# Decoder layer on one core: values' sums in three passes over rounded halves, normalisation on ScalarE, and the table scatters split over two steps

## The reference, cut to what matters

```python
theta_x = einsum('ld,bdt->btl', theta_w, input2) + theta_b
phi_x = einsum('ld,bdt->blt', phi_w, input1) + phi_b[:, None]
p = softmax(einsum('btl,bls->bts', theta_x, phi_x), axis=-1)   # 16 x 512 x 512
g_x = einsum('ld,bdt->btl', g_w, input1) + g_b
t_x = einsum('bts,bsl->blt', p, g_x)                           # the values' sums
# mean and variance of t_x over a whole batch, normalise, gamma, beta, relu
w_t = einsum('ol,blt->bot', out_w, relu(h)) + out_b[None, :, None] + input2
# then, per token: probs = softmax(norm(x) @ Wg), the top 2 of 8 experts, and a
# place below the capacity of each; the place decides the row of a slot table
```

## Time and profile before

| | |
|---|---|
| median of 3 runs | 2969.3 us (2965.92 to 2970.14) |
| the profiled execution | 2979.34 us, its span 2977.6 us |
| mean granted PE clock in it | 0.973 of full |
| PE / DVE / ACT / POOL busy, share of the span | 95 / 42 / 29 / 29 % |
| chain that ended last | PE 61%, nearly all of it in the experts |

### The profile page before, as it was taken

The page is one execution under the profiler, slowest core; times in us unless marked ns, Lnnn a source line. Parts: engine busy times, 40 slices in busy tenths (PEclk is TensorE's granted clock), DMA queues, the critical chain, the costliest instruction groups (busy, mean ns, idle before and its releaser), DMA issues.

```text
span 2977.6 us, 46435 instructions
## 1 busy us (share of the span) xinstructions
PE 2825.9 (95%) x16374; PEld 2310.4 (78%) x16374; DVE 1245.7 (42%) x2129; ACT 870.0 (29%) x1681; POOL 873.7 (29%) x1330
## 2 busy tenths in 40 slices
PE   6989999998999966999999999999999999999998
PEld 6855555556665536999999999999999999999997
DVE  6756777646788752233132133133133133123111
ACT  1126666641544522222122122122122122112110
POOL 4546777622266662021021021021011011111110
PEclk9999999978999977999999999999999999999999
DMA  3101222232121214232033033033023023122110
GB/s 107 42 2 39 44 43 47 54 94 79 57 78 71 78 43 122 68 113 87 11 107 97 11 106 96 11 96 103 12 96 102 19 89 95 30 87 76 36 47 20
DMA packets 97076, 194.66 MB, mean 65 GB/s; under 512 B 22126, under 2 KB 23758, under 8 KB 96800
## 3 DMA queue, kind: packets, MB, share of 16 engines
q1 hardware_dynamic: 75072, 131.77, 14.8%
q0 software_dynamic: 21856, 60.73, 6.6%
HBM read 148.77 MB, written 38.94 MB: 63 GB/s over the span
## 4 chain that ended last, share of the span: by engine, by line
PE 61%; DMA 0%; POOL 0%; DVE 0%; issue 0%; ACT 0%; DVEq 0%; POOLq 0%
PE ex_hid L1751 30%; PE ex_acc L102 10%; PE ex_acc L103 10%; PE ex_acc L104 10%; PE ex_xb L1721 1%; DMA ex_ys<-xn_dram,ex_slot_gather 0%; POOL out_dram L1603 0%; POOL ex_ys L1583 0%; DVE ex_ys L1664 0%; POOL ex_xg L1568 0%; DMA ex_ys<-slot_table_dram 0%; PE ex_acc L1721 0%; DVE ex_h0l L1672 0%; ACT ex_h0h L1631 0%; DVE ex_xT0l L1647 0%
## 5 line engine op out<-in xcount | busy, mean ns | idle before, releaser
L1672 DVE SCALAR_TENSOR_TENSOR ex_h0l<-ex_hid,ex_h0h 128x640 fp32r<-128x640 f32 x128 | 105.6, 825 | 683.1 <-ACT ex_h0h L1631 683.1
L1672 DVE SCALAR_TENSOR_TENSOR ex_h1l<-ex_hid,ex_h1h 128x640 fp32r<-128x640 f32 x128 | 105.5, 824 | 602.8 <-ACT ex_h1h L1631 602.2
L1631 ACT ACTIVATE ex_h0h<-ex_hid 128x640 fp32r<-128x640 f32 x128 | 90.3, 705 | 734.8 <-PE ex_hid L1751 734.8
L1631 ACT ACTIVATE ex_h1h<-ex_hid 128x640 fp32r<-128x640 f32 x128 | 90.3, 705 | 729.6 <-PE ex_hid L1751 729.6
L654 DVE TENSOR_REDUCE at_nb<-at_ring 128x2 f32<-128x512 f32 (+1 forms) x384 | 246.8, 686 | 122.0 <-PE at_ring L760 122.0
L1573 POOL COPY ex_gi<-ex_slot_gather 128x1 int32 (+1 forms) x82 | 15.3, 186 | 916.5 <-PE ex_xb L1721 912.1
L102 PE MATMUL ex_acc<-ex_w_h,ex_h1h 128*128 128x512 f32 x640 | 254.5, 398 | 0.0
L102 PE MATMUL ex_acc<-ex_w_h,ex_h0h 128*128 128x512 f32 x640 | 253.1, 395 | 0.0
L103 PE MATMUL ex_acc<-ex_w_l,ex_h0h 128*128 128x512 f32 x640 | 250.5, 391 | 0.0
L103 PE MATMUL ex_acc<-ex_w_l,ex_h1h 128*128 128x512 f32 x640 | 250.4, 391 | 0.0
L104 PE MATMUL ex_acc<-ex_w_h,ex_h1l 128*128 128x512 f32 x640 | 249.8, 390 | 0.0
(11 more groups left out here) (271 smaller groups left out, 5831.3 us busy)
## 6 DMA issues: line engine op xcount, KB each, us to landing
ex_raw<-in_w_tiles_dram SPq DMA_DIRECT2D x256, 256.0 KB, 2.8
x_in<-in_x_dram SPq DMA_DIRECT2D x32, 256.0 KB, 2.6
act<-at_raw SPq DMA_DIRECT2D x128, 64.0 KB
at_recb<-o_rec_dram SPq DMA_DIRECT2D x16, 512.0 KB
k<-in_x_dram SPq DMA_DIRECT2D x32, 256.0 KB, 2.6
cx_ctx<-in_ctx_dram SPq DMA_DIRECT2D x16, 512.0 KB, 3.6
out_dram<-cx_res SPq DMA_DIRECT2D x16, 512.0 KB, 2.8
xn_dram<-cx_prob SPq DMA_DIRECT2D x16, 512.0 KB, 2.8
```

The lines of the kernel that those rows point to most:

```text
L1631: act.activation(h[f % 2][0][:], hid[:, :, 0:HB], ACT.Relu).then_inc(sm["h_hi"], 1)
L1672: dve.scalar_tensor_tensor(h[f % 2][1][:], hid[:, :, 0:HB], 0.0, f32(h[f % 2][0][:]), ALU.max, ALU.subtract).then_inc(sm["h_lo"], 1)
```

## The change

Values' sums: pT and g's copy are kept as rounded part and remainder (fp32r), the products become three passes; DVE makes the remainders. pT has one buffer instead of two. ACT scales the probabilities (`normalise`), DVE makes only the reciprocals. In odd steps `route_exp` stands ahead of `hid`; the routing's 1/sum moves from POOL's pow to a DVE reciprocal. A group's scatters: six in the even step, the last two in the next odd step after `group_root`. `residual` moves to the end of POOL's step. One more step pair is written out ahead of the loop. SP's program is unchanged.

```diff
-        pT = [s.sb(f"cx_pT{c}", [P, NTT, D]) for c in range(CB)]
+        pT = [s.sb("cx_pT", [P, 2 * NTT, D], F32R)] * CB
-        keys = [s.sb(f"cx_keys{c}", [P, D]) for c in range(CB)]
+        keys = [s.sb(f"cx_keys{c}", [P, 2, D], F32R) for c in range(CB)]
-        LINKS = 26
+        AT_ONCE = 6
+        LINKS = 25
@@ steps
             both(0)
-            with eng.Fori(1, groups - 2) as j:
+            both(1)
+            with eng.Fori(2, groups - 2) as j:
@@ POOL
-                wait_apart(pool, sm["route_exp"], GT * (g + 1), sm["passed_pool"])
-                link(g, TT(exsum[:], exsum[:], minus[:].to_broadcast([P, GT]), ALU.pow))
+                wait_apart(pool, sm["exsum"], g + 1, sm["passed_pool"])
@@ POOL step
                 if within(n - 1, 0, B):
                     group_root(n - 1, 1 - a)
-                if within(n, 0, B):
-                    residual(n, a, j + 1 - a)
+                if within(j - 2, 0, groups - 1) and a == 1:
+                    scatter(j - 2, range(AT_ONCE, TOPK * GT))
...
                 if routed and a == 0:
-                    scatter(j - 1, range(TOPK * GT))
+                    scatter(j - 1, range(AT_ONCE))
+                if within(n, 0, B):
+                    residual(n, a, j + 1 - a)
@@ ACT
+            def normalise(n, c, tiles):
+                for q in tiles:
+                    act.wait_ge(sm["rinv"], ONE + NTT * n + ORDER.index(q) + 1)
+                    act.activation(prob[c][:, q, :], prob[c][:, q, :], ACT.Copy, scale=rinv[:, c, q:q + 1])\
+                        .then_inc(sm["norm"], 1)
@@ ACT step
+                if this:
+                    normalise(n, a, EARLY)
                 if ahead:
                     latent_hi(n + 1, b, "phi")
+                if a == 1 and within(j - 1, 0, groups - 1):
+                    route_exp(j - 1)
                 if last:
                     act.wait_ge(sm["scaled"], ONE + n)
...
-                if a == 1 and within(j - 1, 0, groups - 1):
-                    route_exp(j - 1)
...
                     exponentials(n, a, j + 1 - a, LATE)
+                if this:
+                    normalise(n, a, LATE)
@@ DVE
+            def g_lo(n, c):
+                dve.wait_ge(sm["g_kept"], ONE + n + 1)
+                dve.tensor_tensor(keys[c][:, 1, :], bank[c][2][:], f32(keys[c][:, 0, :]), ALU.subtract)\
+                    .then_inc(sm["g_lo"], 1)
+            def pT_lo(n, c):
+                for q in range(NTT):
+                    dve.wait_ge(sm["pT"], ONE + NTT * n + q + 1)
+                    dve.tensor_tensor(pT[c][:, NTT + q, :], bank[c][q][:], f32(pT[c][:, q, :]), ALU.subtract)\
+                        .then_inc(sm["pT_lo"], 1)
+            def invert_sums(g):
+                wait_apart(dve, sm["route_exp"], GT * (g + 1), sm["passed_dve"])
+                dve.reciprocal(exsum[:], exsum[:]).then_inc(sm["exsum"], 1)
@@ DVE step (both normalise calls become invert_row: the reciprocal alone)
                     for q in LATE:
                         maximum(n, a, q)
+                if ahead:
+                    g_lo(n + 1, b)
+                if a == 1 and within(j - 1, 0, groups - 1):
+                    invert_sums(j - 1)
...
                 if ahead:
                     latent_lo(n + 1, b, "theta")
+                if this:
+                    pT_lo(n, a)
                 if last:
                     dve.wait_ge(sm["rstd"], ONE + n)
@@ PE (theta waits for g_lo instead of g_kept)
                     for q in range(NTT):
-                        pe.wait_ge(sm["pT"], ONE + NTT * n + q + 1)
-                        m = pe.matmul(bank[a][0][:], keys[a][:, q * P:(q + 1) * P], pT[a][:, q, :],
-                                      start=q == 0, stop=q == NTT - 1)
+                        pe.wait_ge(sm["pT_lo"], ONE + NTT * n + q + 1)
+                        m = split_passes(pe, bank[a][0][:], [keys[a][:, i, q * P:(q + 1) * P] for i in range(2)],
+                                         (pT[a][:, q, :], pT[a][:, NTT + q, :]), q == 0, q == NTT - 1)
```

More of the change, by code:

```diff
@@ L910, in stage_cross @@
         least = s.sb("rt_least", [P, E, E])
-        minus = s.sb("rt_minus", [P, 1])
         empty = s.sb("rt_empty", [ST, P, 2], I32)
@@ L920, in stage_cross @@
                  "phi_hi", "phi_lo", "g_kept", "scores", "neg_max", "exp", "rinv", "norm", "turned",
-                 "pT", "tx", "tx_kept", "row_stats", "row_moments", "row_sq", "row_m2", "all_moments",
+                 "pT", "pT_lo", "g_lo", "tx", "tx_kept", "row_stats", "row_moments", "row_sq", "row_m2", "all_moments",
                  "gmv", "gsq", "gvar", "gve", "grstd", "centred", "scaled", "hid", "out", "x2", "stats",
@@ L924, in stage_cross @@
                  "logits_kept", "empty", "consts", "linked", "route_exp", "chosen", "placing",
-                 "placed", "linked_last", "last_slots", "passed_dve", "passed_pe", "passed_pool")
+                 "placed", "exsum", "linked_last", "last_slots", "passed_dve", "passed_pe", "passed_pool")
         sm = {n: s.sem("cx_" + n) for n in names}
@@ L1003, in constants @@
                 pool.iota(empty[:, :, 1], pattern=[[0, P]], base=0, channel_multiplier=0).then_inc(sm["empty"], 1)
-                pool.memset(minus[:], -1.0).then_inc(sm["consts"], 1)
                 pool.memset(acc[:], 0.0).then_inc(sm["consts"], 1)
                 pool.memset(least[:], float(2.0 ** -126)).then_inc(sm["consts"], 1)
-                pool.wait_ge(sm["consts"], ONE + 5)
+                pool.wait_ge(sm["consts"], ONE + 4)
                 for e in range(E):
@@ L1011, in constants @@
                 pool.tensor_copy(tokenf[:], ti[:]).then_inc(sm["consts"], 1)
-                pool.wait_ge(sm["consts"], ONE + 15)
+                pool.wait_ge(sm["consts"], ONE + 14)
                 TS(ec[:], ef[:], float(CAP), None, ALU.mult).then_inc(sm["consts"], 1)
@@ L1015, in constants @@
                     TS(dump[:, k, :], tokenf[:], float(SLOTS + k * B * S), None, ALU.add).then_inc(sm["consts"], 1)
-                pool.wait_ge(sm["consts"], ONE + 18)
+                pool.wait_ge(sm["consts"], ONE + 17)
                 every = [P, NT, E]
@@ L1020, in constants @@
                        dump[:, k, :].unsqueeze(2).to_broadcast(every), ALU.subtract).then_inc(sm["consts"], 1)
-                pool.wait_ge(sm["consts"], ONE + 20)
+                pool.wait_ge(sm["consts"], ONE + 19)
             def route_rank(g):
@@ L1129, in keep_g @@
                 act.wait_ge(sm["g"], ONE + n + 1)
-                act.activation(keys[c][:], bank[c][2][:], ACT.Copy).then_inc(sm["g_kept"], 1)
+                act.activation(keys[c][:, 0, :], bank[c][2][:], ACT.Copy).then_inc(sm["g_kept"], 1)
             def exponentials(n, c, i, tiles):
@@ L1214, in maximum, with invert_row @@
                     .then_inc(sm["neg_max"], 1)
-            def normalise(n, c, q):
+            def invert_row(n, c, q):
                 dve.wait_ge(sm["exp"], ONE + NTT * n + ORDER.index(q) + 1)
                 dve.reciprocal(rinv[:, c, q:q + 1], rsum[:, c, q:q + 1]).then_inc(sm["rinv"], 1)
-                dve.wait_ge(sm["rinv"], ONE + NTT * n + ORDER.index(q) + 1)
-                dve.tensor_scalar(prob[c][:, q, :], prob[c][:, q, :], rinv[:, c, q:q + 1], None, ALU.mult)\
-                    .then_inc(sm["norm"], 1)
+            def g_lo(n, c):
[7 more added lines that the diff above has]
+                        .then_inc(sm["pT_lo"], 1)
             def keep_logits(n, c):
@@ L1255, in step @@
                     for q in EARLY:
-                        normalise(n, a, q)
+                        invert_row(n, a, q)
                 if last:
@@ L1363, in _ @@
                 xin_lo(c, c)
-            for name in ("phi", "theta"):
-                latent_lo(0, 0, name)
+            latent_lo(0, 0, "phi")
+            g_lo(0, 0)
+            latent_lo(0, 0, "theta")
             steps(dve, step)
@@ L1372, in theta @@
                 pe.wait_ge(ctx_loaded[c], ONE + 16 * i + 16)
-                pe.wait_ge(sm["g_kept"], ONE + n + 1)
+                pe.wait_ge(sm["g_lo"], ONE + n + 1)
                 for k in range(TPB):
```

## The result

The change made the kernel slower: 3013.7 us (median of 4 runs, 3010.52 to 3019.93) against 2967.6, a ratio of 1.0159 with a 95% interval of 1.0145 to 1.0172. (The kernel before has a fourth run here, so its median is 2967.6 and no longer 2969.3.) The forecast was 2970.4, the range ended at 2984.

A forecast was written before the change was run, and what follows sets the result against it. PE was taken to bound even steps, and its wait for `hid` behind POOL's scatters to lengthen odd ones. Even steps +3.0, odd -2.75, ends -4.75 and clock +5.6 gave +1 on 2969.3: 2970.4 us, range 2952 to 2984.

The forecast's parts named there:

- the even step's term: Even steps: DVE's remainders outweigh PE's 0.66 us saving, so each takes 19.95 us against 19.45, +3.0 over six.
- 5.6 for the clock: Odd steps: PE's longer idle may lower its clock; half of 2.77 us, taken as 1.4, in four of five steps.
- the other steps and both ends: Steps 0 and 1 -0.6, step 3 +0.1, step 14 0.45 less, step 15 3.8 less: -4.75 us together.
- `hid` and L1277: Odd step: L1277 falls to 0.75 us, `hid` is ready at +9.55, and PE's wait of 3.23 us goes.
- SP's three transfers: Odd step: context load, x2 store and xn3 store start together at +7.5, held until the even step's `residual` ends.
- I take 13.1: Odd step: first LATE exponential waits for both stores until 7.5 + 1.4 + 4.2 = +13.1, against +14.46 today.
- the bound of 14.1: Odd step: latest landing of the stores, 7.5 + 6.6 us, the 6.6 being one transfer of 1536 KB.
- costs POOL and DVE what it does today: Port shared by POOL and DVE, odd step: no added cost from the change.
- The values' passes: Values' sums on PE: twelve passes take 0.66 us less, but PE waits about 1.5 us for DVE's pT remainders in even steps.
- given back by `residual`: Odd step: the 2.5 us of two scatters moved out are offset by `residual` now standing ahead of the next `group_root`.
- rival A: Odd steps: PE's clock falls at the values' passes and transposes, 17.8 less 4.5: +13, 2982 us; chance 0.30.
- a gain elsewhere is not to be had: Whole kernel: the change touches only the stage at 728 to 1120 us, 392 us of a span of 2977.6.

## Why the prediction was wrong

The step that failed first is the even step's term. I gave the six even steps 0.5 us each, +3.0, and they took +19.0: the odd step's residual now ends inside them, so the same three transfers hold the late exponential, the passes begin with the first remainder and end later, a held square stands on PE's path, and in two of them the clock falls. Second, the odd step's transfers were sized too small, and third, the experts stood in no term and lost 14.2. By the forecast's own frame:

| part of the stage | before | after | change | forecast |
|---|---|---|---|---|
| six even steps, 2 to 12 | 116.3 | 135.3 | +19.0 | +3.0 |
| five odd steps, 5 to 13 | 119.7 | 127.3 | +7.6 | +2.85 (-2.75, and 5.6 for the clock) |
| the other steps and both ends | 162.7 | 160.8 | -1.9 | -4.75 |

These are 23.6 us over the forecast, 16.0 of them in the even steps. With the experts' 14.2 that is 37.8 of the 43 that the medians lie above it; the rest is no more than how far the profiled executions lie from their medians. (The ends of the range, 2952 and 2984, are 1 and 2 us wider than the words beside them give.)

The change put together, one step after another, from the table of versions (each within about 3 us, and in this order only):

| step | cross | experts |
|---|---|---|
| before | 398.7 | 1850.9 |
| pair written out | +2.2 | -1.6 |
| scatters split | -13.9 | +1.6 |
| ACT normalises | -13.6 | -1.2 |
| route's exponential and reciprocal | -3.2 | +0.2 |
| three passes | +20.2 | +12.4 |
| residual last | +33.0 | +2.8 |
| after | 423.4 | 1865.1 |

- **`hid` and L1277: right.** The wait went, `scaled` takes 0.74 us in all steps, `hid` is ready at +10.0 (9.55 forecast).
- **SP's three transfers: right in place, wrong in size.** They are issued at +7.3 to +8.5 as forecast. The exponential starts at +15.0; "I take 13.1" fails, and so does the bound of 14.1, which came from one transfer of 1536 KB. In step 11 three transfers started together landed in 4.3 (load), 4.9 and 6.4 us (the stores), where a load had 3.6 and a store 2.8 alone; from the load's issue to the exponential that is 7.7 us, and 9.3 in step 9. The estimate of 5.6 us by the Trainium skill ("DMA: Bandwidth & Descriptors", "Anatomy of one DMA") is further off than the row of 6.6; the skill gives that sum there for GpSimd's path, a condition that the prediction left out, and these transfers are SP's.
- **The even step was given no such wait: the largest omission.** I moved only the even step's residual. The odd step's lands in the even step at +1.8 to +4.2, its load and stores at +4.3 to +5.5, and the late exponential waits 1.3 us (974.62, +11.3). Of the ten waits for the stores five are in even steps, 9.5 of the 31.4 us.
- **The port: "costs POOL and DVE what it does today" failed.** The large operation was freed (2.83 to 0.74), but the small ones with two SBUF inputs now meet the residual: 1.90 us on PE's path to `avg` in even steps, 2.98 on POOL's path to `grstd` in odd ones, 0.16 before. PE's waits for the mean matmul's operand rose from 1.6 us in 1 to 5.4 in 6.
- **The values' passes: mechanism right, size off.** PE waits 1.4 us a step for the first remainder on average, as forecast (1.5), and up to 2.65. But I let the last remainder decide, at 18.35 plus three passes. In the version with the residual early the first remainder starts the passes at +16.9, and the twelve take 2.86 from there: the step ends at 20.6, not at 19.95. Even steps pay 1.1, not 0.5. The prediction's own rows said so: three passes take 0.69, a remainder 0.60, so the passes and not the remainders set the end.
- **What the parts were worth without each other I did not ask.** Split and normalisation save 27 us together. I called the split "given back by `residual`" and ACT's scalings "nothing"; what either is worth beside the late residual no run shows. Step 1 gained 4.0 us (its clock went from 0.78 to 1.00), where I had 0.6 for steps 0 and 1.
- **The clock: rival A was partly right.** The stage's mean is 0.90, as before, but the low level lies elsewhere. In steps 5, 9, 11 and 13 it falls behind waits of 3.1 to 5.2 us for ACT's rows, at the transposes (3.4 to 3.6 us instead of 1.91). In steps 3, 4, 6 and 7 it falls at the values' passes, as rival A had it, behind waits of 2.0 to 2.65 us for the first remainder: there twelve passes take 4.4 to 5.3 us, 7.1 more in all. Two of these steps are even; for them the forecast had no clock term, though the rival named the case. Its gaps were mis-added too: 13.2 to 15.65 and 17.4 to 20.1 are 5.15 us of missing work, not 4.4.
- **The experts: "a gain elsewhere is not to be had" said nothing of a loss.** The new code on PE was counted as instructions, not as a shift of what follows: 14.2 us, of them 10.3 of stalls (the five) and 3.7 of PE busy time at the lower clock behind two of them.

## What to carry to other kernels

Moving an operation to the end of an engine's step moves everything that a queue holds behind it, in every kind of step, and transfers that were spread then go together: a wait that is hidden today is part of the price. When a change bundles parts, cost each one alone; here two good parts, worth 27 us together, were bundled with the three passes (20 us, and 12 more in the experts by where they move the code) and the residual's place (33). A loop that nobody touched can lose 0.5% when code ahead of it grows: look at PE's idle time that ends on its own issue, and at the instruction queue's packets, before explaining such a loss by data.

## What was not expected of the hardware

- A VectorE subtraction of one column took up to 2.98 us beside a GpSimd addition of 128x1024, ending when that ended, and 3.15 us when that was cut into two that follow each other; 0.16 us otherwise.
- PE stood still for 1.9 to 2.4 us once per turn of a loop of some 230 us, in kernels whose loop had the same instructions as others that did not, and 32 small transposes ahead of the loop took this away.
- Three transfers of 512 KB issued within 1.2 us took 7.7 us (step 11) until the engine that waited for them went on. In slices of 0.25 us the DMA view shows 393 to 418 GB/s over 2.5 us of it, no more than the 418 of a load by itself (before, step 9), and only 90 to 303 in the 2 us ahead of that.
